# One merged transfer for the small tables, shared weights in quarters, and the routing's VectorE steps between the first shared units

## The reference, cut to what matters

```python
rw = softmax(router_logits)                 # cond_8: 16 sequences x 8 experts
w, sel = top_k(rw, 2);  w = w / w.sum()
w = w / 12 + (1 - 1 / 12) * w
out = sum over the 2 chosen experts e: w[e] * mlp(x, gate[e], up[e], down[e])
out = out + mlp(x, shared_gate, shared_up, shared_down)
mlp(x, g, u, d) = (gelu(x @ g) * (x @ u)) @ d          # inner width 512
```

## Time and profile before

| | |
|---|---|
| median of 3 runs | 533.54 us (532.94 to 533.87) |
| the profiled execution, its own time | 532.82 us |
| its span, first to last instruction | 531.0 us |
| TensorE matmul busy | 445.4 us, 84% |
| VectorE busy | 423.8 us, 80% |
| ScalarE busy | 241.4 us, 45% |
| GpSimd busy | 54.2 us, 10% |
| mean granted TensorE clock | 0.937 of full speed |
| chain that ended last | TensorE 66%, VectorE 26%, issue 5%, ScalarE 2% |

### The profile page before, as it was taken

How to read it: one execution, slowest core, us unless ns; L and a number is a source line. 1 busy time by engine, 2 the same in 40 slices (tenths; PEclk the granted TensorE clock), 3 DMA queues, 4 the chain that set the end, 5 groups by cost and what they waited for, 6 DMA issues and landing times.

```text
span 531.0 us, 8982 instructions
## 1 busy us (share of the span) xinstructions
PE 445.4 (84%) x3474; PEld 302.8 (57%) x3474; DVE 423.8 (80%) x883; ACT 241.4 (45%) x406; POOL 54.2 (10%) x69
## 2 busy tenths in 40 slices
PE   3999978999799969200799989999999999999653
PEld 1448968997258744100389975567555656555310
DVE  6989999886765659999825568756998998997987
ACT  5678736562472239883554753235223223321200
POOL 3050000000092006300180000000000000000000
PEclk9999989999799999755799988999999999999999
DMA  7991967910081004203320000069820000000000
GB/s 213 419 396 66 317 235 252 328 60 0 1 251 67 1 1 153 85 0 124 115 89 1 2 1 1 1 190 397 314 71 7 6 5 7 6 11 6 6 15 10
DMA packets 20353, 56.13 MB, mean 106 GB/s; under 512 B 2596, under 2 KB 5031, under 8 KB 20311
## 3 DMA queue, kind: packets, MB, share of 16 engines
q1 hardware_dynamic: 19872, 55.46, 30.0%
q10 hardware_dynamic: 438, 0.11, 0.1%
HBM read 53.36 MB, written 1.15 MB: 103 GB/s over the span
## 4 chain that ended last, share of the span: by engine, by line
PE 66%; DVE 26%; issue 5%; ACT 2%; DMA 0%; DVEq 0%; ACTq 0%
PE bk L654 15%; PE bk L662 8%; DVE XT L1472 7%; DVE QS L1240 5%; PE bk L365 5%; PE bk L699 5%; PE bk L387 4%; PE bk L360 4%; PE bk L595 2%; DVE RC L993 2%; PE bk L549 2%; PE bk L471 1%; PE bk L480 1%; PE bk L508 1%; DVE RA L1310 1%
## 5 line engine op out<-in xcount | busy, mean ns | idle before, releaser
L1472 DVE SCALAR_TENSOR_TENSOR XT<-bk,WK,XT 128x128 f32<-128x128 f32 x256 | 89.1, 350 | 8.8 <-PE bk L699 0.4
L654 PE MATMUL bk<-X,RB 128*128 128x512 f16 x384 | 94.9, 384 | 0.0
L910 ACT ACTIVATE X<-RA 128x512 f16<-128x512 f32 x64 | 40.1, 630 | 104.9 <-DVE RA L1487 83.5
L699 PE MATMUL bk<-RB,RA 128*128 128x512 f16 x192 | 51.7, 380 | 12.5 <-DVE XT L1472 9.8
L654 PEld LDWEIGHTS bk<-X,RB 128*128 128x128 f16 x384 | 36.7, 99 | 44.3 <-issue 4.5
L662 PEld LDWEIGHTS bk<-RB,X 128*128 128x128 f16 x768 | 48.9, 99 | 15.4 <-issue 0.6
L662 PE MATMUL bk<-RB,X 128*128 128x128 f16 x768 | 54.0, 220 | 0.0
L365 PE MATMUL bk<-X,RC 128*128 128x128 f16 x768 | 47.9, 219 | 2.0 <-DVE RC L993 1.8
L365 PEld LDWEIGHTS bk<-X,RC 128*128 128x128 f16 x768 | 45.2, 98 | 4.1 <-issue 3.4
L1460 DVE TENSOR_TENSOR X<-RA,X 128x512 f16<-128x512 f32 x64 | 43.8, 685 | 1.9 <-ACT X L910 1.9
L765 ACT ACTIVATE WK<-bk 128x512 f32<-128x512 f32 x48 | 28.6, 596 | 28.8 <-PE bk L365 20.8
(11 more groups left out here) (285 smaller groups left out, 774.1 us busy)
## 6 DMA issues: line engine op xcount, KB each, us to landing
RA<-in_wx SPq DMA_DIRECT2D x27, 768.0 KB, 5.9
RC<-expert_weights SPq DMA_DIRECT2D x22, 256.0 KB, 6.3
X<-in_w SPq DMA_DIRECT2D x8, 512.0 KB, 3.5
RC<-in_wx SPq DMA_DIRECT2D x5, 768.0 KB, 6.1
RC<-in_w SPq DMA_DIRECT2D x8, 384.0 KB, 4.2
STG<-in_w SPq DMA_DIRECT2D x6, 384.0 KB, 6.7
WBOT<-expert_weights SPq DMA_DIRECT2D x8, 256.0 KB, 6.6
STG<-expert_weights SPq DMA_DIRECT2D x6, 256.0 KB, 8.8
```

What stands on the lines that cost most here:

```text
L654: t = e.matmul(BK[m][:, :], P16[:, wp, wo:wo + 128], ZH[:, n % 4, xp, :], start=(e1 == 0 and i == 0), stop=(e1 == 15 and i == 2))
L699: t = e.matmul(bank_o(n)[:, :], OT16[:, xp, bb_(4 * c + b)], P16[:, wp, 6144 + 512 * g:6656 + 512 * g], start=(i == 0), stop=(i == 2))
L910: e.activation(ZH[:, r, 0, :], zf[r], ACT.Copy).then_inc(S("z_hi"), 1)
L1472: stt(XT[:, bb_(t_)], bank_o(n)[:, bb_(i)], RW[:, t_, e1:e1 + 1], XT[:, bb_(t_)], ALU.mult, ALU.add).then_inc(S("acc"), 1)
```

## The change

`condB`, the old `pka`, `cols` and `c2b` become one table `pka` of 330 columns (165 KB), third in SyncE's queue; `bv` goes to the end of that queue's first run. ScalarE issues no transfer any more. The shared weights come, and are split, in a quarter (`j` = 0), a quarter (`j` = 1) and a half. On VectorE the splits of quarter 0, chunk 0 and quarter 1 come first; then the maximum and the subtraction for the exponential (`EXP_IN` is now 2), four routing steps, and the split of the half. The other routing steps run behind the units, three each behind the first four. One step for the second expert's exponential is now a product and a sum in place of a subtraction and an exponential, so the chain has 30 steps for 29. Chunks 1 to 3 of `x` are split behind units 0 to 2.

```diff
-PKA = {"iota8": (0, 128), "gates": (128, 144)}
+PKA = {"cond": (0, 128), "iota8": (128, 256), "gates": (256, 272), "cols": (272, 290), "c2b": (290, 330)}
+        SHARES = (slice(0, 384), slice(384, 768), slice(768, 1536))
-        ROUTED, EXP_IN, WEIGHTS, BIASES = 13, 15, 24, 29
+        EXP_IN, FIRST, ROUTED, WEIGHTS, BIASES = 2, 6, 14, 25, 30
...
-                    q.wait_ge("sh_lo", j // 2 + 1)
+                    q.wait_ge("sh_lo", min(j, 2) + 1)
...
-            e.dma_start(PKAT[:, :], A["pka"]).then_inc(S("pka"), 16)
-            e.dma_start(COL[:, :], A["cols"]).then_inc(S("col"), 16)
-            e.dma_start(C2B[:, :, :], A["c2b"]).then_inc(S("c2b"), 16)
-            e.dma_start(BV[:, :], A["bv"]).then_inc(S("bv"), 16)
...
             sh_hi(0)
             x_hi(0)
+            sh_hi(1)
             q.wait_ge("route", EXP_IN)
             e.activation(sl8(5), sl8(4), ACT.Exp).then_inc(S("route_exp"), 1)
-            e.activation(sm(5), sm(4), ACT.Exp).then_inc(S("route_exp"), 1)
             q.wait_ge("theta0", 1)
             e.activation(QS[:, 1:2], QS[:, 0:1], ACT.Exp).then_inc(S("theta"), 1)
-            sh_hi(1)
-            x_hi(1)
+            sh_hi(2)
...
-                if k < 2:
-                    x_hi(2 + k)
+                if k < 3:
+                    x_hi(1 + k)
...
             def first_max(lg, m, eq, ix, oh):
-                red(m, lg, X_AX, ALU.max).then_inc(route.next(), 1)
-                then(route)
                 tt(eq, lg, over8(m), ALU.is_equal).then_inc(route.next(), 1)
+                yield
...
-            first_max(CONDB[:, :, :], sm(0), sl8(0), sm(1), sl8(1))
-            stt(sl8(2), sl8(1), NEG, CONDB[:, :, :], ALU.mult, ALU.add).then_inc(route.next(), 1)
-            then(route)
-            first_max(sl8(2), sm(2), sl8(0), sm(3), sl8(3))
...
-            assert route.n == ROUTED
-            tt(sl8(4), CONDB[:, :, :], over8(sm(0)), ALU.subtract).then_inc(route.next(), 1)
-            tt(sm(4), sm(2), sm(0), ALU.subtract).then_inc(route.next(), 1)
...
-            sh_lo(0)
-            x_lo(0)
-            q.wait_ge("col", 16)
-            ts(QS[:, 0:1], col("theta"), 0.0, None, ALU.mult).then_inc(S("theta0"), 1)
-            sh_lo(1)
-            x_lo(1)
...
             def routing():
+                yield from first_max(CONDB, sm(0), sl8(0), sm(1), sl8(1))
+                assert route.n == FIRST
...
+                stt(sl8(2), sl8(1), NEG, CONDB, ALU.mult, ALU.add).then_inc(route.next(), 1)
...
+                red(sm(2), sl8(2), X_AX, ALU.max).then_inc(route.next(), 1)
...
+                yield from first_max(sl8(2), sm(2), sl8(0), sm(3), sl8(3))
...
+                ts(EIX[:, :, :], SM[:, 1:4:2, :], 99.0, 128.0, ALU.add, ALU.mult).then_inc(route.next(), 1)
+                assert route.n == ROUTED
...
+                q.wait_ge("route_exp", 1)
+                tt(sl8(0), sl8(5), sl8(3), ALU.mult).then_inc(route.next(), 1)
...
+                red(sm(5), sl8(0), X_AX, ALU.add).then_inc(route.next(), 1)
...
             ahead = routing()
+            sh_lo(0)
+            x_lo(0)
+            sh_lo(1)
+            q.wait_ge("pka", 16)
+            red(sm(0), CONDB, X_AX, ALU.max).then_inc(route.next(), 1)
+            then(route)
+            tt(sl8(4), CONDB, over8(sm(0)), ALU.subtract).then_inc(route.next(), 1)
+            assert route.n == EXP_IN
+            ts(QS[:, 0:1], col("theta"), 0.0, None, ALU.mult).then_inc(S("theta0"), 1)
+            for _ in range(4):
+                next(ahead)
+            sh_lo(2)
...
-                if k < 2:
-                    x_lo(2 + k)
+                if k < 3:
+                    x_lo(1 + k)
-                for _ in range(2):
+                for _ in range(3 if k < 4 else 2):
                     next(ahead, None)
...
-            q.wait_ge("route", 5)
-            q.wait_ge("c2b", 16)
+            q.wait_ge("route", FIRST)
+            q.wait_ge("pka", 16)
...
-            e.dma_start(CONDB[:, :, :], A["condB"]).then_inc(S("cond"), 16)
-            e.dma_start(SHW[:, 0:768], A["w0"][:, 0:768]).then_inc(S("sh0"), 16)
+            e.dma_start(SHW[:, SHARES[0]], A["w0"][:, SHARES[0]]).then_inc(S("sh0"), 16)
             e.dma_start(XT[:, cc(0)], A["xT"][:, cc(0)]).then_inc(S("x0"), 16)
-            e.dma_start(SHW[:, 768:1536], A["w0"][:, 768:1536]).then_inc(S("sh1"), 16)
+            e.dma_start(PKAT[:, :], A["pka"]).then_inc(S("pka"), 16)
+            for h in (1, 2):
+                e.dma_start(SHW[:, SHARES[h]], A["w0"][:, SHARES[h]]).then_inc(S(f"sh{h}"), 16)
             for c in range(1, 4):
                 e.dma_start(XT[:, cc(c)], A["xT"][:, cc(c)]).then_inc(S(f"x{c}in"), 16)
+            e.dma_start(BV[:, :], A["bv"]).then_inc(S("bv"), 16)
```

More of the change, by code:

```diff
@@ L67 @@
     (("cent", 4), ("root", 6), ("whole_max", 5), ("nm", 8)),
-    (("const", 2), ("sh_lo", 2), ("sim_sq", 1), ("ffs", 4), ("k_out", 4)),
+    (("const", 2), ("sh_lo", 3), ("sim_sq", 1), ("ffs", 4), ("k_out", 4)),
     (("x_lo", 4), ("xq", 4), ("quant", 12), ("ot_lo", 4)),
-    (("route", 29), ("router", 70), ("rw", 4)),
+    (("route", 30), ("router", 70), ("rw", 4)),
     (("chosen", 5), ("l1p", 1), ("relm", 1), ("cos", 32), ("p16", 8)),
@@ L142, in program @@
         PK1T = sb("PK1T", [128, PK1N])
-        PKAT = sb("PKAT", [128, 144])
+        PKAT = sb("PKAT", [128, 330])
         PK2T = sb("PK2T", [128, 384])
-        COL = sb("COL", [128, len(COLS)])
-        C2B = sb("C2B", [128, 5, 8])
         BV = sb("BV", [3, 256])
@@ L181, in col @@
         def col(n):
-            return COL[:, CI[n]:CI[n] + 1]
+            return pka("cols")[:, CI[n]:CI[n] + 1]
         def cc(c):
@@ L215, in program @@
         iota8 = pka("iota8").rearrange("p (b e) -> p b e", e=8)
+        CONDB = pka("cond").rearrange("p (b e) -> p b e", e=8)
+        C2B = pka("c2b").rearrange("p (k e) -> p k e", e=8)
         ge = [WK[:, 1, 512 * i:512 * i + 512] for i in range(3)]
@@ L736, in sh_hi @@
                 q.wait_ge(f"sh{h}", 16)
-                o = 768 * h
-                e.activation(W16[:, o:o + 768], SHW[:, o:o + 768], ACT.Copy, scale=WS).then_inc(S("sh_hi"), 1)
+                e.activation(W16[:, SHARES[h]], SHW[:, SHARES[h]], ACT.Copy, scale=WS).then_inc(S("sh_hi"), 1)
             def gu_hi(u):
@@ L987, in sh_lo @@
                 q.wait_ge("sh_hi", h + 1)
-                o = 768 * h
-                stt(W16[:, 1536 + o:2304 + o], SHW[:, o:o + 768], WS, W16[:, o:o + 768], ALU.mult, ALU.subtract).then_inc(S("sh_lo"), 1)
+                low = slice(1536 + SHARES[h].start, 1536 + SHARES[h].stop)
+                stt(W16[:, low], SHW[:, SHARES[h]], WS, W16[:, SHARES[h]], ALU.mult, ALU.subtract).then_inc(S("sh_lo"), 1)
             def gu_lo(u):
@@ L1710, in layout @@
             c[q + w + "s"] = g[a + q + w][sw]
-    A["cols"] = np.stack([c[k] for k in COLS], 1)
     d = "L1_cond2_b_"
-    A["c2b"] = np.stack([g[d + "up"][:, :128].T, g[d + "up"][:, 128:].T, g[d + "gate"][:, :128].T, g[d + "gate"][:, 128:].T, g[d + "down"].T], 1)
+    c2b = np.stack([g[d + "up"][:, :128].T, g[d + "up"][:, 128:].T, g[d + "gate"][:, :128].T, g[d + "gate"][:, 128:].T, g[d + "down"].T], 1)
+    A["pka"] = np.concatenate([np.broadcast_to(g["cond_8"].reshape(1, 128), (128, 128)), np.broadcast_to(np.tile(np.arange(8, dtype=f) - 99, 16)[None], (128, 128)),
+                               np.broadcast_to(g["L1_ffn_gates"][None], (128, 16)), np.stack([c[k] for k in COLS], 1), c2b.reshape(128, 40)], 1)
     A["bv"] = np.broadcast_to(g[a + "bv"][None], (3, 256))
```

20 lines of the change are left out of this document (14 added, 6 removed).

## The result

| | before | after |
|---|---|---|
| median of 13 runs each | 533.57 us | 535.24 us |
| lowest and highest | 532.88 to 534.31 | 533.41 to 536.57 |
| ratio, 95% interval | | 1.0026 (1.0014 to 1.0039) |
| the profiled execution | 532.82 us, span 531.0 | 533.41 us, span 531.6 |

The changed kernel is 0.26% slower, some 1.4 us by the ratio. Its profiled execution happens to be the fastest of its 13.

The account below looks back on a forecast made before the run. TensorE was taken to bound the kernel from 9.19 to 36 us, VectorE to 46.85, TensorE to about 56, then VectorE. Terms -0.2 + 1.5 + 0.2 on 532.82 gave 534.3; +0.7 for the median, -0.2 for slow matmuls: 534.8 (532.0 to 536.2).

Parts of the forecast that it names:

- Transfers: First loads, by bytes ahead in the queue: chunk 0 lands at 4.7 us, quarter 1 at 5.9, bounds 5.0 and 6.8.
- First "gated": VectorE's first "gated", after a 4.8 us chain from quarter 1's landing: starts at 10.7 us, before at 12.58.
- VectorE behind it: Units 0 to 3 with routing steps, chunk splits and GpSimd's products beside: 9.9 us on VectorE, against 7.2 before.
- TensorE against it: First five `down`: TensorE stalls 1.3 us ahead of the first, starts the fifth at 23.9, before 24.11; worth -0.2.
- The move past SyncE's queue: First expert weight issued at 20.9 us, everything behind it in the queue 11.2 later; weights still in time.
- GpSimd's product: `L1W * L1M` moves to near 43.5 us, where VectorE sets the time, and stops it: +1.5 us, bounds 1.0 to 1.8.
- The small operations: Eleven GpSimd operations behind the product move to a stretch where VectorE is all but full: +0.2 us, 0 to 0.6.
- The slow first matmuls: First 24 matmuls, some 2.1 us slow, leave the path as TensorE has time in hand before `down(0)`: -0.2 us.
- Rival A: Routing steps fit between the first units without holding TensorE, so all 3.0 us at the first matmul stays: 532.2; chance 0.1.
- Rival B: GpSimd's product falls behind 46.85 us, where TensorE sets the time, and costs 0.5: 533.8; chance 0.3.
- C: Late landings: quarter 1 at 6.8 us puts the first "gated" and all behind it 0.9 later: 535.7; chance 0.15.
- D: Early landings: quarter 1 at 5.0 us, first "gated" at 9.8, and a cheap product: 532.9; chance 0.12.

Follow-up runs that it names:

- Experiment 9: Changed kernel with its merged table loaded in four transfers, as before the change; 535.43 us, ratio 1.0033.
- experiment 6: Changed kernel with one routing step behind each of units 0 to 3, chunk splits behind units 1, 4, 8, product at the 45th `up`; 532.19 us, ratio 0.9961.
- experiment 1: Changed kernel with GpSimd's 128x1024 product and the small operations behind it held back to the 36th `up`; 535.12 us, ratio 1.0027.
- experiment 2: Changed kernel with GpSimd's 128x1024 product held back to the 45th `up`, near 120 us; 533.52 us, ratio 0.9990.
- experiments 5: Changed kernel with one routing step behind each of units 0 to 3, chunk splits behind units 1, 4, 8, product at the 36th `up`; 534.01 us, ratio 1.0006.
- experiment 7: Changed kernel with one routing step behind each of units 0 to 3, GpSimd's product left where `l1m` lands; 532.49 us, ratio 0.9988.
- Experiment 3: Kernel before with only GpSimd's product made to wait for the 18th `up`, as late as in the changed kernel; 535.91 us, ratio 1.0032.
- experiment 4: Kernel before with GpSimd's product and the small operations behind it moved to the 45th `up`; 533.36 us, ratio 1.0000.
- experiment 8's first run: Changed kernel with one routing step behind each of units 0 to 3, product at the 36th `up`, packed tables issued ahead of the `ROUTED` wait; 532.88 us, ratio 0.9987.

## Why the prediction was right

Forecast 534.8 (532.0 to 536.2), measured 535.24: +1.7 by the medians, +1.4 by the ratio, against a forecast of +1.3. The mechanism was the one described in its two main parts: a head that is worth nothing because VectorE can't follow, and a product that stops VectorE where VectorE sets the time. In the profile the parts add up to +0.1 for the head, -0.25 for the small operations and +1.5 for the product, 1.37 in all; the forecast had -0.2, +0.2 and +1.5. The head came out by luck in part, since two errors of about 1 us cancel in it. The sizes, in the order of the steps:

- *Transfers.* The weakest step. Chunk 0 landed at 1.19 + 4.4 = 5.6, not 4.7. Quarter 1 landed at 7.04, not 5.9, and beyond my upper bound of 6.8: 387 KB fewer saved 0.88 us, where the rate of the full queue gave 1.1. Experiment 9 shows that bytes are a poor measure here. The same 805 KB in other pieces moved quarter 1 by 0.3, and 64 KB more ahead of chunk 0, with three short tables beside it, moved that by 1.15.
- *First matmul* 7.13, not 6.2: all of it from the landing.
- *First "gated"* 11.81, not 10.7. From quarter 1's landing it is 4.8 us, to the tenth what the chain summed to.
- *VectorE behind it* 9.05 for four units, not 9.9. The routing steps overlap the next operation by more than I allowed, and GpSimd's five products took 2.71 us in all and cost `x_lo` 0.16 and hardly more; I had charged 0.6. The first unit alone took 2.22 instead of 2.7.
- *TensorE against it.* The fifth `down` at 24.22, not 23.9. The two errors, 1.1 late and 0.85 short, nearly cancel. The stall ahead of the first `down`, forecast at 1.3, was 0.25 in this profile and 1.34 and 1.27 in those of experiments 1 and 2, whose 24 matmuls took 6.95 and 7.09. That the head is worth nothing although TensorE starts 2 us earlier was right, and experiment 6 shows that VectorE's load is the reason: with the load spread, 1.9 us are there at the fifth `down`.
- *The move past SyncE's queue.* First issue at 21.55, forecast 20.9; `l1m` 11.6 later, forecast 11.2. ScalarE waited for no weight in this kernel. In experiments 5 to 7, where they are issued 2 to 3 us later still, it did.
- *GpSimd's product.* At 43.92, forecast 43.5; the stop of `h_lo` 1.5, forecast 1.5; TensorE 1.37 late. Without the 0.25 that the small operations gave back, and from a head 0.11 late, that is 1.5. Experiments 2 and 3 show it from both sides: taking the product away from there removes the loss, and putting it there in the kernel before makes it.
- *The small operations.* I gave them +0.2 at their new place, where they cost nothing to be seen: TensorE stays 1.37 late from 48 to beyond 90 us. What I had put at nothing is their leaving the old place, and that gave 0.25 back (experiment 4). Experiment 2 has it too: from 0.25 late at the fifth `down` to level at 46.85.
- *The slow first matmuls.* I gave 0.2 for their leaving the path. The changed kernel's 24 took 7.99 us in its profile and 6.93 in experiment 9's, and in both the next `down` waited for `h_lo`. In the kernel before they are on the path: in experiment 4's profile 24 took 8.02, and the `down` behind them came at once. Why this doesn't show as a gain in the median is not settled.

Rival A (VectorE keeps up) fell by the first profile. Rival B (a cheap product) is refuted for 44 us, and experiment 7 shows that it was near: three microseconds later, the condition that B names, the profile's price is the 0.5 that B gives, though the medians show more. C was true as to the landing, but its 0.9 was eaten by VectorE's shorter sum. D did not occur.

One thing was not in the forecast. The executions of the changed kernel lie between 533.4 and 536.6, more than twice as wide as the 13 of the kernel before beside them, though 35 of the kernel before beside experiments 1 and 3 span 2.7. In the two profiles TensorE's granted clock in the same stretches differs. The profiles by stretch, before and then after (length, busy time of each engine, granted clock, DMA):

```profile
305.00:335.00 30.00, 28.43 (x190) 18.78 (x189) 22.97 (x69) 13.24 (x30) 0.00 (x0) 0.83 0.01 1
```

```profile
305.00:335.00 30.00, 28.43 (x197) 19.57 (x197) 23.01 (x71) 15.18 (x33) 0.00 (x0) 0.89 0.01 1
```

Here the profile after was granted 0.89 where before was granted 0.83, levels of 2.4 and 1.2 GHz mixed, and TensorE got back 1.35 of the 2.0 us by which it was late ahead of this stretch; 0.7 of the 2.0 it had lost at 257 us, where 36 matmuls took 9.99 instead of 9.29. So in this profile some 0.7 of the loss is hidden, and its execution is only 0.6 slower than before's, while the medians differ by 1.7. The forecast's 534.3 for the profiled execution was 0.9 too high, most of it for the same reason.

The width doesn't go with the product's place. Experiment 3, with the product at 44 us, lies between 533.6 and 537.6, but experiment 9, with it there too, only between 534.9 and 536.6, and experiment 8's first run, with it near 92, between 531.1 and 535.3. In the changed kernel the width goes with the mean granted clock of the execution: the four longest, 536.1 to 536.6, were granted 0.931, and the three shortest, 533.4 to 534.0, were granted 0.939. Why the clock differs from one execution to the next is open.

## What to carry to other kernels

Work that another engine starts when a transfer lands is moved by whatever moves the queue. Before an issue is delayed, list what each of its transfers sets off, and what that will meet at the new time. A wait that pins such work to a place where the engine it collides with has idle time to spare costs next to nothing (experiment 2), but "TensorE sets the time" doesn't mean that VectorE is idle (experiment 1).

An earlier start of the leading engine is worth only what the engine behind it can follow: sum that engine's work per unit, and put the optional steps where it has slack.

## What the runs showed of the hardware that was not expected

- VectorE's operations with both inputs in SBUF stood still until GpSimd's product was over, in five places: 1.88, 2.20, 2.52, 2.70 and 2.72 us instead of 0.68 to 1.22, each ending 0.5 to 1.1 after it. "Gated", with one input in PSUM, kept its 0.75 beside it.
- Three short tables on ScalarE's queue and 64 KB more ahead on SyncE's delayed the landing of a 256 KB transfer by 1.15 us (5.63 to 6.78), 0.46 of it by the later issue. In each case one profile.
- The first 24 matmuls took between 6.76 and 8.15 us in twelve profiles, whose first matmul started between 6.85 and 9.52 us. They are on the path only where TensorE doesn't wait behind them: in the changed kernel the fifth `down` started at 24.08 to 24.36 with 6.95 to 7.99 (profiles of experiments 1 and 2 and its own), while in experiments 5 and 7 it moved from 21.42 to 22.96 with 6.76 and 8.15.
